# A decoder layer on one core: a new hand-written order of all engines, the last two chunks' transposes read in PSUM, and filler matmuls up to the first exp unit

## The reference

```python
x = layernorm(x + attention(x))        # 32 query heads of 8 channels, 8 key/value heads, softmax over 256 keys
x = layernorm(x + wkv(w, u, x, ctx))   # a recurrence over the 256 rows, k = x, v = ctx
x = layernorm(x + ffn(x))
# wkv, per channel: running maximum o, weighted sums p (with v) and q (without)
#   no = max(o, u + k);  A = exp(o - no);  E = exp(u + k - no);  y = (A p + E v) / (A q + E)
#   no2 = max(w + o, k); p = exp(w+o-no2) p + exp(k-no2) v;  q likewise;  o = no2
# ffn: h = relu(x @ up)^2 @ down  +  (x @ expert_weight) * (sum of the two largest of x @ gate)
#      then a layernorm of its own with gamma and beta
```

## Time and profile before

| what | us |
|---|---|
| three timed runs | 208.05, 207.22, 207.79 |
| their median | 207.79 |
| the profiled execution, its own time | 205.89 |
| its span, first to last instruction | 203.8 |
| what lies around the span in it | 2.09 |

### The profile page before, as it was taken

The page is one execution under the profiler, slowest core; times in us unless marked ns, Lnnn a source line. Parts: engine busy times, 40 slices in busy tenths (PEclk is TensorE's granted clock), DMA queues, the critical chain, the costliest instruction groups (busy, mean ns, idle before and its releaser), DMA issues.

```text
span 203.8 us, 4423 instructions
## 1 busy us (share of the span) xinstructions
PE 190.7 (94%) x1311; PEld 112.3 (55%) x1311; DVE 171.4 (84%) x422; ACT 155.9 (76%) x344; POOL 119.9 (59%) x231
## 2 busy tenths in 40 slices
PE   7999999999998999999999999999999989999960
PEld 3744343344423345657474656854673677898940
DVE  7887977897999999799999899988968596876663
ACT  6741587878998989889899889989988974683630
POOL 8806356707557483564573848677499368365731
PEclk9999999999999999999999999999999999999998
DMA  6212623362120309000321020000030000000010
GB/s 212 97 51 57 238 58 84 79 225 61 50 68 26 87 8 326 8 24 0 79 67 45 2 61 0 8 3 8 26 84 3 0 0 27 3 2 27 26 51 26
DMA packets 13415, 11.76 MB, mean 58 GB/s; under 512 B 3664, under 2 KB 11344, under 8 KB 13136
## 3 DMA queue, kind: packets, MB, share of 16 engines
q1 hardware_dynamic: 13248, 11.35, 18.6%
q10 hardware_dynamic: 144, 0.13, 0.3%
HBM read 6.57 MB, written 1.05 MB: 37 GB/s over the span
## 4 chain that ended last, share of the span: by engine, by line
PE 68%; DVE 17%; issue 6%; ACT 4%; POOL 3%; POOLq 0%; DVEq 0%; ACTq 0%
PE ps_heads L693 11%; PE ps_max L664 9%; PE ps_b L855 8%; PE ps_b L872 7%; PE ps_exp L677 7%; DVE maxima L1287 7%; PE ps_a L813 4%; DVE top L1376 3%; PE ps_exp L855 3%; PE ps_b L838 2%; PE ps_a L767 2%; PE ps_a L756 2%; PE ps_heads L872 2%; PE ps_exp L705 2%; DVE den L1400 2%
## 5 line engine op out<-in xcount | busy, mean ns | idle before, releaser
L1287 DVE TENSOR_REDUCE maxima<-ps_max 128x2 f32<-128x512 f32 x128 | 82.1, 681 | 9.0 <-PE ps_max L664 8.5
L906 ACT ACTIVATE probs<-ps_exp 128x512 f32<-128x512 f32 x128 | 70.8, 596 | 10.1 <-PE ps_exp L677 9.5
L664 PE MATMUL ps_max<-k_rows,q_rows 64*128 64x256 bf16 x256 | 39.6, 272 | 1.6 <-DVE maxima L1287 1.1
L677 PE MATMUL ps_exp<-q_rows,k_rows 64*128 64x512 bf16 x128 | 37.9, 383 | 0.7 <-ACT probs L906 0.6
L693 PE MATMUL ps_heads<-probs,v_cols 128*32 128x512 f32 x256 | 33.9, 604 | 0.0
L1159 POOL TENSOR_TENSOR rstd<-var_eps,minus_half 128x1 f32<-128x1 f32 x32 | 18.7, 583 | 22.9 <-DVE var_eps L1252 22.8
L664 PEld LDWEIGHTS ps_max<-k_rows,q_rows 64*128 64x128 bf16 x256 | 14.7, 94 | 27.8 <-DVE maxima L1287 19.2
L872 PE MATMUL ps_b<-down_sb,inner_t 128*128 128x256 f32 x112 | 26.9, 381 | 0.0
L855 PE MATMUL ps_b<-x_t,up_sb 128*128 128x128 f32 x192 | 25.3, 279 | 0.6 <-DVE h L1476 0.4
L855 PEld LDWEIGHTS ps_b<-x_t,up_sb 128*128 128x128 f32 x192 | 23.1, 192 | 2.6 <-ACT relu_t L1041 1.3
L872 PEld LDWEIGHTS ps_b<-down_sb,inner_t 128*128 128x128 f32 x112 | 20.3, 190 | 2.7 <-issue 0.3
(11 more groups left out here) (153 smaller groups left out, 356.3 us busy)
## 6 DMA issues: line engine op xcount, KB each, us to landing
q_rows<-q_parts SPq DMA_DIRECT2D x42, 64.0 KB, 2.0
x_t<-in_x_cols SPq DMA_DIRECT2D x4, 256.0 KB, 3.9
x_in<-in_x SPq DMA_DIRECT2D x4, 256.0 KB, 2.9
ctx_t<-in_ctx_cols SPq DMA_DIRECT2D x4, 256.0 KB, 3.0
up_sb<-in_up_w SPq DMA_DIRECT2D x1, 1024.0 KB, 5.5
down_sb<-in_down_w SPq DMA_DIRECT2D x1, 1024.0 KB, 5.4
out_y<-y_out SPq DMA_DIRECT2D x8, 128.0 KB, 1.7
post_sb<-in_w_post SPq DMA_DIRECT2D x1, 906.0 KB, 5.5
```

Source lines behind the costliest of these rows:

```text
L664: last = nc.tensor.matmul(ps_max[n % 2][:, r, :], q_rows[b][at:at + HALF, g, REP * jj + 2 * half + r, h * P:h * P + P], k_rows[b][at:at + ...
L677: nc.tensor.matmul(ps_exp[n % 2][:, :], k_rows[b][at:at + HALF, JH * g + jj, kt * P:kt * P + P], q_rows[b][at:at + HALF, g, REP * jj:REP * ...
L906: nc.scalar.activation(probs[n % 8][:, :], ps_exp[n % 2][:, :], ACT.Exp, scale=SCALE).then_inc(s_exp, 1)
L1287: nc.vector.tensor_reduce(maxima[s % 2][:, g, j // JH, 0, at:at + 2], ps_max[n % 2][:, :, :], AX, ALU.max, negate=True).then_inc(s_max, 1)
```

## The change

1. **Order.** All ticks of `AT` are new. Counted as ranks on each engine, 236 of TensorE's 455 steps change place, by 1.0 places in the mean over all; 195 of VectorE's 338 (1.5); 194 of ScalarE's 321 that remain (1.5); 142 of GpSimd's 167 (3.6); and 50 of SP's 68 (2.5), loads, row copies and stores. No step moves to another engine.
2. **Kept transposes.** For chunks 6 and 7 `x1_e` is gone (tick -1). The scans and `del` read the transposes in `ps_a` instead of `x1_t`. `kept` marks these uses: who waits for such a use of the bank to be read now waits until both `del` of that chunk are done.
3. **Offsets.** `neg_mean` and its semaphore are gone. GpSimd computes the offset in one instruction as mean times rstd times -1.
4. **Fillers.** A filler now follows any maxima unit, `k`, `q` (of sequences 1 and up) or `m` step whose tick lies from the fourth maxima unit up to the first exp unit. By the new ticks (47 to 81) these are maxima units 3 to 12, m0.0, k.1 and q0.1: 13 in all.

The diff, with the order table cut to the steps that are spoken of:

```diff
@@ -47,173 +47,172 @@
...
     AT = {
-        "load": (1, 2, 9, 107, 113, 114, 274, 489, 560, 563, 589, 768, 910, 1162),
-        "k": (3, 66, 125, 301),
-        "q0": (4, 82, 152, 363),
...
-        "qc12": (70, 249, 459, 706),
...
-        "m0": (75, 174, 283, 393, 525, 685, 844, 991),
...
-        "mc0": (83, 176, 309, 410, 539, 691, 876, 1017),
...
-        "hn": (221, 367, 504, 584, 741, 930, 1062, 1183),
...
-        "pow0": (288, 475, 638, 643, 800, 979, 1108, 1216),
...
-        "x1": (318, 499, 650, 692, 818, 1013, 1121, 1218),
-        "x1_e": (319, 500, 659, 711, 819, 1023, 1127, 1220),
-        "top0": (327, 513, 661, 718, 847, 1033, 1128, 1225),
-        "top1": (343, 518, 660, 722, 836, 1044, 1134, 1226),
-        "del0": (351, 534, 662, 725, 852, 1035, 1135, 1227),
-        "del1": (352, 533, 667, 739, 863, 1045, 1137, 1228),
-        "re0": (360, 535, 677, 747, 898, 1046, 1147, 1235),
...
-        "ex0": (404, 546, 693, 772, 903, 1065, 1163, 1236),
...
-        "yn0": (436, 618, 780, 826, 954, 1117, 1185, 1257),
...
-        "st1": (486, 647, 805, 889, 1054, 1160, 1209, 1287),
...
-        "nor1": (511, 669, 828, 900, 1083, 1168, 1224, 1290),
-        "x2": (512, 676, 833, 917, 1103, 1175, 1229, 1298),
...
-        "x2b": (554, 670, 1148, 1196, 1232, 1233, 1234, 1297),
...
-        "up2": (591, 761, 846, 965, 1173, 1222, 1242, 1308),
-        "up3": (592, 771, 859, 966, 1177, 1238, 1243, 1319),
...
-        "down0_3": (675, -1, 1064, -1, 1215, -1, 1299, -1),
-        "h3": (687, 845, 1077, 1120, 1221, 1284, 1312, 1340),
-        "expert1": (-1, 688, -1, 992, -1, 1252, -1, 1301),
...
+        "load": (1, 9, 51, 52, 53, 112, 289, 291, 527, 552, 712, 782, 783, 822),
+        "k": (2, 68, 114, 304),
+        "q0": (3, 78, 144, 370),
...
+        "qc12": (50, 255, 311, 409),
...
+        "m0": (66, 168, 286, 397, 530, 688, 848, 995),
...
+        "mc0": (81, 199, 288, 406, 557, 717, 853, 1005),
...
+        "hn": (225, 372, 507, 574, 732, 925, 1054, 1186),
...
+        "pow0": (309, 492, 616, 654, 791, 997, 1115, 1203),
...
+        "x1": (324, 503, 645, 692, 817, 1018, 1126, 1213),
+        "x1_e": (325, 506, 656, 704, 819, 1027, -1, -1),
+        "top1": (339, 519, 657, 707, 820, 1037, 1136, 1220),
+        "del1": (340, 533, 665, 711, 855, 1038, 1145, 1222),
+        "top0": (358, 514, 660, 710, 821, 1034, 1139, 1221),
+        "del0": (359, 518, 666, 724, 854, 1035, 1140, 1223),
...
+        "re0": (398, 547, 668, 726, 857, 1049, 1146, 1232),
...
+        "ex0": (416, 549, 682, 744, 938, 1050, 1155, 1233),
...
+        "yn0": (469, 626, 758, 801, 1014, 1109, 1190, 1250),
...
+        "st1": (501, 647, 804, 886, 1085, 1156, 1211, 1279),
...
+        "nor1": (511, 663, 828, 902, 1088, 1170, 1216, 1289),
+        "x2": (520, 673, 836, 903, 1111, 1171, 1224, 1294),
...
+        "up2": (588, 756, 850, 972, 1164, 1237, 1242, 1313),
+        "up3": (615, 778, 851, 973, 1165, 1238, 1282, 1315),
...
+        "down0_3": (675, -1, 1067, -1, 1218, -1, 1296, -1),
+        "h3": (678, 824, 1077, 1128, 1219, 1274, 1307, 1340),
+        "expert1": (-1, 689, -1, 999, -1, 1251, -1, 1325),
...
+        "x2b": (871, 872, 908, 909, 1275, 1310, 1319, 1330),
...
@@ -347,7 +346,6 @@
         mean_var = [sb(f"mean_var{i}", [P, TT, 2]) for i in range(4)]
         var_eps = [sb(f"var_eps{i}", [P, TT]) for i in range(4)]
         rstd = [sb(f"rstd{i}", [P, TT]) for i in range(4)]
-        neg_mean = [sb(f"neg_mean{i}", [P, TT]) for i in range(4)]
         offset = [sb(f"offset{i}", [P, TT]) for i in range(4)]
 
         ps_max = [ps(f"ps_max{i}", [P, 2, T]) for i in range(2)]
@@ -396,7 +394,6 @@
         s_heads, s_headst, s_att = sem("s_heads"), sem("s_headst"), sem("s_att")
         s_xbo = sem("s_xbo")
         s_var = [sem(f"s_var{k}") for k in range(4)]
-        s_negmean = [sem(f"s_negmean{k}") for k in range(4)]
         s_rstd = [sem(f"s_rstd{k}") for k in range(4)]
         s_offset = [sem(f"s_offset{k}") for k in range(4)]
         s_x1 = by_class("s_x1")
@@ -438,9 +435,17 @@
                         [(name, p) for name in ("att", "op", "x1", "yt", "x2") for p in range(NC)])
         A_USE = {use: i for i, use in enumerate(A_BY)}
 
+        def kept(name, p):
+
+            return name == "x1" and p >= WIDE
+
         def a_done(engine, use):
 
-            engine.wait_ge(s_a_read, A_USE[use] + 1)
+            if kept(*use):
+                for c in range(CT):
+                    engine.wait_ge(s_delta[c], use[1] + 1)
+            else:
+                engine.wait_ge(s_a_read, sum(not kept(*v) for v in A_BY[:A_USE[use] + 1]))
 
         def a_filled(engine, use):
             engine.wait_ge(s_a, A_USE[use] + 1)
@@ -694,7 +699,10 @@
                                             probs[(4 * n + j) % 8][:, :], start=(i == 0), stop=(i == 2 * NSET - 1))
                 last.then_inc(s_pv, 1)
 
-            def keep_busy():
+            def keep_busy(tick):
+
+                if not AT["score_max"][3] <= tick < AT["score_exp"][0]:
+                    return
                 pe.wait_ge(s_krow0, 1)
                 pe.wait_ge(s_qrow0, 2)
                 nc.tensor.matmul(ps_exp[0][:, :], k_rows[0][0:HALF, 0, 0:P], q_rows[0][0:HALF, 0, 0:REP, P:2 * P],
@@ -716,8 +724,8 @@
                 n = SCORE_MAX.get(tick)
                 if n is not None:
                     maxima_unit(n // UNITS, n % UNITS)
-                    if n in RAMP:
-                        keep_busy()
+                    if n < 2 * UNITS:
+                        keep_busy(tick)
                 for kp, done in enumerate((s_k1, s_k2, s_k3)):
                     if AT["ksel"][kp] == tick:
                         pe.wait_ge(done, 1)
@@ -756,6 +764,8 @@
                             last = nc.tensor.matmul(ps_a[:, 0:T], wkv_cols[:, c, :], x_t[b][:, c, :],
                                                     start=(c == 0), stop=(c == CT - 1))
                         last.then_inc(s_a, 1)
+                        if b >= 1:
+                            keep_busy(tick)
                     for g in range(NSET):
                         if AT[f"q{g}"][b] == tick:
                             if b == 0:
@@ -1159,10 +1172,9 @@
                             gp.tensor_tensor(rstd[k][:, ti], var_eps[k][:, ti], minus_half[:, ti],
                                              ALU.pow).then_inc(s_rstd[k], 1)
                             if p < WIDE:
-                                gp.wait_ge(s_negmean[k], p + 1)
                                 gp.wait_ge(s_rstd[k], p + 1)
-                                gp.tensor_tensor(offset[k][:, ti], neg_mean[k][:, ti], rstd[k][:, ti],
-                                                 ALU.mult).then_inc(s_offset[k], 1)
+                                gp.tensor_scalar(offset[k][:, ti], mean_var[k][:, ti, 0], rstd[k][:, ti], -1.0,
+                                                 ALU.mult, ALU.mult).then_inc(s_offset[k], 1)
                     for half in range(2):
                         if AT[f"nv{half}"][p] == tick and (half == 1 or p < WIDE):
                             gp.wait_ge(s_ctx[b], 16)
@@ -1251,9 +1263,6 @@
                 settle()
                 nc.vector.tensor_scalar(var_eps[k][:, ti], mean_var[k][:, ti, 1], EPS, None,
                                         ALU.add).then_inc(s_var[k], 1)
-                if p < WIDE:
-                    nc.vector.tensor_scalar(neg_mean[k][:, ti], mean_var[k][:, ti, 0], -1.0, None,
-                                            ALU.mult).then_inc(s_negmean[k], 1)
 
             def normalise(k, p, src, dst, done):
                 dve.wait_ge(s_rstd[k], p + 1)
@@ -1368,22 +1377,24 @@
                         normalise(0, p, h1, x1[b % 2], s_x1[p >= WIDE])
                     for c in range(CT):
                         if AT[f"top{c}"][p] == tick:
-                            a_done(dve, ("x1", p))
+                            (a_filled if kept("x1", p) else a_done)(dve, ("x1", p))
+                            src = ps_a[:, c * n:c * n + n] if kept("x1", p) else x1_t[:, c, cols]
                             if p == 0:
                                 dve.wait_ge(s_w_post, 16)
                                 dve.wait_ge(s_const, B + 4)
                             settle()
                             own(nc.vector.tensor_tensor_scan(top[:, c, t0 + 1:t0 + n + 1],
                                                              decay_sb[:, c:c + 1].broadcast_to([P, n]),
-                                                             x1_t[:, c, cols], scan_from(top, c, p, NEG),
+                                                             src, scan_from(top, c, p, NEG),
                                                              ALU.add, ALU.max))
                         if AT[f"del{c}"][p] == tick:
                             settle()
+                            src = ps_a[:, c * n:c * n + n] if kept("x1", p) else x1_t[:, c, cols]
                             if before(p):
```

(2 more changed lines are left out.)

82 lines of the change are left out of this document (38 added, 44 removed), and 193 rows, old and new, of the table AT.

## The result

| | before | after |
|---|---|---|
| median of the runs shown, us | 207.5 (207.15 to 208.05, 4 runs) | 213.5 (211.01 to 215.87, 4 runs) |
| profiled execution: time, span, mean granted clock | 205.89, 203.8, 0.996 | 211.01, 209.0, 0.974 |
| ratio of after to before | | 1.0246, 95% interval 1.0176 to 1.0317 |
| T, the end of the output projection of chunk 7 | 168.98 | 173.02 |
| last matmul | 196.87 = T + 27.9 | 202.07 = T + 29.05 |

The change is slower by 6.0 us in the medians and by 5.1 us in the profiled executions, well outside the range.

What follows compares the result with a forecast made beforehand. Bound: TensorE and VectorE nearly full up to 150 us, chunk 5 and 6 chains to 169, then TensorE alone. Terms +1.8 - 0.7 + 0.1 - 0.4 - 0.7 = +0.1 gave 207.9, lowered 0.3 to 207.6 us; range 205.0 to 209.6.

Steps and rivals of the forecast that it cites:

- Start and fillers: Kernel start: two more fillers cost +0.1 us; the first exp unit about 0.6 us earlier gives -0.4 at the end.
- if the first exp unit comes after 21.5: Kernel start: a sign that the forecast is wrong; the first exp unit was expected near 20.0 us.
- The order up to T: Up to the end of op.7: reordering fills a sixth of 4.4 us of TensorE idle time, -0.7 us.
- Retained transposes, cost: Behind op.7: TensorE stands still about 2.6 us before x2.6 until both del finish; +1.8 us, bounds +0.9 to +2.4.
- Retained transposes, source: Scans and del of chunks 6 and 7: reading PSUM instead of SBUF makes no difference, bounds -0.1 and +0.3 us.
- Saving: Chunks 6 and 7: dropping two ScalarE copies of 387 ns saves 0 to 0.3 us on the path; taken as 0.
- Offsets: VectorE: 24 instructions removed, 19 before T; half of 19 x 0.07 us counted, -0.7 us, bounds 0 and -2.7.
- Medians: Whole kernel: the sum for one profiled execution, 206.0 us, carried to the runs' median by adding 1.9 us.
- The rivals: Alternatives to the forecast case (0.40): more won before T, 205.9 us (0.33); kept bank decides (0.27); parts do nothing.
- The kept bank decides: Rival, chance 0.27: full standstill at x2.6, mc0.0's copy behind the loads, T unmoved; +1.8 us, 209.6 us.

Runs made afterwards that it cites:

- e16: e1 with no filler matmul at all (14 taken away); 208.25 us, ratio 0.9994 to the kernel before.
- e1: The order of before with the change's other three parts (kept transposes, offsets, new filler rule giving 14 fillers); 207.5 us, ratio 1.0038.
- e13: e7 with SyncE's queue alone put back in the order of before; 206.37 us, ratio 0.9966.
- e15: e1 with `qm1.0` late on ScalarE, as in the change, and its remainder behind the second maxima unit on VectorE; 207.76 us, ratio 1.0028.
- e5: The changed kernel with the two ScalarE copies of the transposes of chunks 6 and 7 put back; 208.94 us, ratio 1.0123.
- e2: The changed kernel with fillers behind maxima units 3 to 12 only, 10 instead of 13; 210.41 us, ratio 1.014.
- e7: The changed kernel with the start and everything behind op.7 in the order of before, only the middle new; 207.13 us, ratio 1.001.
- e17: e13 with the two ScalarE copies of the transposes put back; 206.33 us, ratio 0.9982.
- e6: The changed kernel with the steps behind op.7 in the order of before, start and middle new; 211.29 us, without a ratio.
- e4: The changed kernel with the start in the order of before, all later steps new; 210.5 us, ratio 1.0161.
- e9: The changed kernel with `qm1.0` moved behind the last two evictions of query rows on ScalarE; 214.78 us, ratio 1.0391.
- e11: The changed kernel with e9's move and `k.1` moved ahead of maxima units 8 and 9 on TensorE; 216.0 us, ratio 1.0272.
- e14: The changed kernel with `qm1.0` moved ahead of the first evictions of key rows on ScalarE; 209.98 us, ratio 1.0105.
- e18: e14 with `k.1` also moved ahead of maxima units 8 and 9 on TensorE; 209.84 us, ratio 1.0121.
- e8: e1 with only the start in the new order, middle and tail in the order of before; 210.58 us, ratio 1.0139.
- e12: The changed kernel with the order of before up to exp unit 32 and behind op.7, new order between; 210.74 us, ratio 1.0208.

## Why the prediction was wrong

**Start and fillers (term +0.1 and -0.4): the step that failed.** "The clock is 1.00 [...] so fillers can win nothing in this execution" took the clock as given. It was at its upper level because the old start, with its fillers, kept it there, as e16 shows beside e1, e13 and e15: without them the mean clock is low in ten of twelve executions, with them in none of 34. A reordered start had to be asked whether it still keeps it. In 11 of 14 executions with the new start and at least the new middle the mean clock was low, and the fall costs 3.0 us at the first exponential and 3.1 us at T (the change against e5). The first exp unit did come earlier where the clock held, 20.49 in e5 against 20.64, though not by the 0.6 us forecast. Three more fillers than the ten of e2 were not what broke it, and 26 were as costly as the fall. The text named the sign that it would be wrong ("if the first exp unit comes after 21.5"), but gave that case no chance and no price.

**The order up to T (term -0.7): the gain did not come.** Where the clock held, T was 169.9 (e5), where the terms together gave 167.2. So T came at + 0.9 instead of - 1.7. Apart from two loads at the start, the sum left out the 50 moved steps of SyncE. Its order costs 0.7 us by unit 32 (28.6 us from the first exponential in e7, 27.9 in e13 and e17); the theory of e13 claimed 2. No SyncE row on the chain of before says that it was not the bound, not how near it stood to being one: its queue was nearly without a gap from 25.6 to 42.2 us. What the rest of the order gains stays open.

**Retained transposes, cost (term +1.8): mechanism right, size too large.** 2.19 us of standstill against 2.6, last matmul at T + 29.05 against T + 29.8: +1.15 us, inside the bounds of +0.9 to +2.4. e5, e6 and e17 split it: 0.5 us goes when the copies return or when the old tail returns, 0.6 more when both do. The step lacked its second price: in the profiled executions of e4, e9 and e11 the clock fell behind the standstill of 2.19 us, 1.6 us more in the tail (30.66 against 29.03); in six others with the same standstill it did not. The Trainium skill's advice in "PSUM — Partial Sum Buffer" (summary of rules for kernel authors), to evacuate promptly, fits the wait of 2.19 us at x2.6, though the page gives PSUM's small size as its reason, and here it is one bank with one user at a time.

**Retained transposes, source (0).** Right: the medians from PSUM and SBUF lie within 8 ns of each other, in the rows above. The dearer PSUM source of the Trainium skill's "VectorE: DVE Perf Modes" (errata section), an estimate of +0.5 us from its figures, does not show in these rows.

**Saving (0).** Nothing contradicts it: the times of e13 and e17 are not told apart.

**Offsets (-0.7).** Not tested by itself. e1 holds old order, offsets and fillers together and is not faster than before (T 170.1 against 169.0), so no 0.7 us shows, though a mark of one execution would not resolve it. GpSimd's instruction took 264 ns against the 224 used. It stays open.

**Medians.** In the profiled execution the loss adds up: 3.1 us for the clock at the start, 0.9 for what else changed up to T (which two profiled executions of like kernels can differ by as well), 1.15 behind T. The sum was made for one execution and carried over by the same 1.9 us. That assumes the spread stays. It did not: the profiled execution of the change is the best of its four, and the others had clocks of 0.945 to 0.966. That is more time at the lower level than this one fall; where it lay is not on record.

**The rivals.** "The kept bank decides" gave 209.6 and named the side, but its mechanism is 1.15 us of the 5.1, and 1.6 us more where the clock falls behind it. The clock, 3.1 of the 5.1 us in the profiled execution, was in none of them.

**What stays open.** Which property of the new start lets the clock fall. A wait of 0.43 us near 13 us goes with it, and with 1.80 us the mean clock was low in all six executions of e9 and five of six of e11. But e5 with the short wait and e11 with the long one kept their clock at the start in the profiled executions, e15 failed to make the wait in the old start, and neither `k.1` nor `qm1.0` back in its place, nor both, restored it, though falls were fewer with `qm1.0` early (8 of 19 in e14 and e18 against 11 of 14), which is too little to call shown. The loads, which now run from 13 to 17 us, were not moved back by themselves. In e8 two of the three are issued behind 18 us and the clock fell all the same; the third, at 13.7 us, is an open rival. The best kernel found, e13, is 0.34% below before with an interval that just reaches 1; e17 beside it is not told apart.

## What to carry to other kernels

A clock that reads 1.00 all along is a result of the schedule, not a property of the chip: before you move the first dense work of a kernel, or take out or add matmuls that nobody reads, ask what holds it, and time enough executions, since it can fall in some and not in others. An engine that is off the chain, even one that only issues transfers, can be nearly full; when an order is rewritten, look at its queue like any other, and at which of its steps another engine waits for. A standstill of TensorE costs its length and then perhaps a stretch at half speed behind it: here 2.19 us, and behind it 1.6 us more in three of nine profiled executions.

## What the runs showed that I had not expected

- The same instructions with the same busy time before 17 us ended in a lower clock in one execution (the change, 0.50 from 18 to 24 us) and not in another (e5, 1.00). A fall to 0.967 in the mean costs 4.9 us in e14, nearly what the mean clock says.
- The clock fell behind standstills of 2.2 and 3.2 us in the middle and the tail as well: at 176 us in e4, 181 in e9, 178 in e11, 61 in e12. It also fell with no standstill over 0.4 us in the few us before: at 29 us in e8, at 47 in e18. And it held at the start of e11 through 1.81 us.
- 26 fillers put the first exponential as late (23.8 us) as half the clock for 7 us did (23.9). None at all cost little in the median of the times (208.25 against 207.5, not run side by side).
- A copy's issue takes SyncE 0.59 us, and a run of 23 of them sets the pace of a kernel whose TensorE is 92% busy (the change, e7) or stays off the chain (before, e13), by their order.
